# Where quarter B12 stands in the second pair of token tiles, and when the third sum of weights is formed

## What is computed

```python
def _L0_ffn_ref(x, W_base, b_base, W_gate, W_thr, b_thr, A_w, B_w):
    ...
    base = jnp.einsum('bsd,od->bso', x, W_base) + b_base
    xf = x.reshape(-1, D)
    gate = jax.nn.softmax(xf @ W_gate.T, axis=-1)
    thr = jax.nn.sigmoid(xf @ W_thr + b_thr[0]) * MAX_THRESHOLD
    adapted = gate - thr[:, None]
    selected = (adapted >= 0).astype(x.dtype)
    w = adapted * selected
    wsum = jnp.sum(w, axis=-1, keepdims=True)
    wsum = jnp.where(wsum == 0, jnp.ones_like(wsum), wsum)
    w = w / wsum
    h = jnp.einsum('nd,erd->ner', xf, A_w)
    moe = jnp.einsum('ner,ne,eor->no', h, w, B_w) * SCALING
    return base + moe.reshape(base.shape)
...
x = x + jnp.tanh(g_xattn[0]) * _L0_xattn_ref(_layernorm(x, axis=-1), ctx_4096, ...)
x = x + jnp.tanh(g_ffn[0]) * _L0_ffn_ref(_layernorm(x, axis=-1), ...)
```

## Time and profile before

| | us |
|---|---|
| median of three runs | 489.45 (488.79 to 489.53) |
| the profiled execution, its own time | 489.19 |
| its span, first to last instruction | 487.1 |
| PE busy in the span | 473.6 |
| DVE busy in the span | 345.9 |
| ACT busy, POOL busy | 164.6, 127.5 |

### The profile page before, as it was taken

The page is one execution under the profiler, slowest core; times in us unless marked ns, Lnnn a source line. Parts: engine busy times, 40 slices in busy tenths (PEclk is TensorE's granted clock), DMA queues, the critical chain, the costliest instruction groups (busy, mean ns, idle before and its releaser), DMA issues.

```text
span 487.1 us, 6840 instructions
## 1 busy us (share of the span) xinstructions
PE 473.6 (97%) x2460; PEld 402.2 (83%) x2460; DVE 345.9 (71%) x720; ACT 164.6 (34%) x338; POOL 127.5 (26%) x113
## 2 busy tenths in 40 slices
PE   4999999999999999999999999999999999999997
PEld 3888899998888888888888887877888888888885
DVE  1267758563787867769977996988767679777742
ACT  3765312310214204227326325244151422414300
POOL 1011011002353353336152515514040401305000
PEclk9999999999999999999999999999999999999999
DMA  8962262027843368557669035040503113050202
GB/s 291 412 247 87 88 250 96 1 87 253 266 137 123 150 215 283 199 200 249 208 257 399 4 131 215 27 146 2 172 3 129 45 60 113 1 173 1 86 0 87
DMA packets 20160, 71.80 MB, mean 147 GB/s; under 512 B 2464, under 2 KB 3488, under 8 KB 18848
## 3 DMA queue, kind: packets, MB, share of 16 engines
q1 hardware_dynamic: 19984, 71.35, 40.8%
q10 hardware_dynamic: 144, 0.02, 0.0%
HBM read 56.69 MB, written 14.68 MB: 147 GB/s over the span
## 4 chain that ended last, share of the span: by engine, by line
PE 79%; DVE 11%; issue 4%; DMA 3%; ACT 2%; POOL 0%; SPq 0%; DVEq 0%; ACTq 0%; POOLq 0%
PE bank L706 8%; PE bank L710 8%; PE bank L708 8%; PE bank L558 6%; PE bank L623 6%; PE bank L625 6%; PE bank L624 6%; PE bank L588 3%; PE bank L590 3%; PE bank L589 3%; PE bank L686 3%; PE bank L487 2%; DVE wl_T L1316 2%; DMA out_dram<-xs 2%; PE bank L609 2%
## 5 line engine op out<-in xcount | busy, mean ns | idle before, releaser
L1430 POOL TENSOR_TENSOR small<-small,tiny 128x1 f32<-128x1 f32 (+2 forms) x25 | 23.6, 945 | 150.3 <-DVE small L1079 124.1
L623 PE MATMUL bank<-xth,gram 128*128 128x512 f32 x144 | 57.4, 398 | 0.0
L625 PE MATMUL bank<-xtl,gram 128*128 128x512 f32 x144 | 56.3, 391 | 0.0
L624 PE MATMUL bank<-xth,gram 128*128 128x512 f32 x144 | 56.1, 390 | 0.0
L1404 DVE SCALAR_TENSOR_TENSOR xs<-bank,tiny,xs 128x512 f32<-128x512 f32 x56 | 40.2, 747 | 21.6 <-PE bank L710 15.7
L706 PE MATMUL bank<-wh_B,zh 128*128 128x512 f32 x136 | 55.2, 406 | 0.0
L710 PE MATMUL bank<-wh_B,zl 128*128 128x512 f32 x136 | 53.5, 393 | 0.0
L708 PE MATMUL bank<-wl_B,zh 128*128 128x512 f32 x136 | 53.3, 392 | 0.0
L1458 POOL TENSOR_TENSOR sq_sum<-sq_sum,sq 128x512 f32<-128x512 f32 x24 | 32.0, 1332 | 62.7 <-DVE sq L1252 62.7
L1494 POOL TENSOR_TENSOR xs<-xs,bb 128x1024 f32<-128x1024 f32 x16 | 39.5, 2468 | 10.3 <-ACT zn L946 7.7
L706 PE MATMUL bank<-wh_T,zh 128*128 128x512 f32 x96 | 39.3, 410 | 1.8 <-DVE wl_T L1316 1.6
(11 more groups left out here) (185 smaller groups left out, 1111.5 us busy)
## 6 DMA issues: line engine op xcount, KB each, us to landing
xst<-x_dram SPq DMA_DIRECT2D x16, 512.0 KB, 3.6
xz<-xt_dram SPq DMA_DIRECT2D x16, 512.0 KB, 6.8
out_dram<-xs SPq DMA_DIRECT2D x14, 512.0 KB, 3.0
xa<-x_dram SPq DMA_DIRECT2D x12, 512.0 KB, 3.3
x<-xa SPq DMA_DIRECT2D x12, 512.0 KB, 2.6
xs<-x SPq DMA_DIRECT2D x12, 512.0 KB, 4.0
wq_raw<-wq_dram SPq DMA_DIRECT2D x8, 512.0 KB, 14.9
wr_B<-wb_dram SPq DMA_DIRECT2D x4, 1024.0 KB, 8.5
```

Source lines behind the costliest of these rows:

```text
L623: pe.matmul(acc[:, :], gram[:, g, 0, :], xth[b % 2][:, r, :], start=r == ROWS[j][0], stop=False)
L624: pe.matmul(acc[:, :], gram[:, g, 1, :], xth[b % 2][:, r, :], start=False, stop=False)
L625: done = pe.matmul(acc[:, :], gram[:, g, 0, :], xtl[b % 2][:, r, :], start=False, stop=r == ROWS[j][-1])
```

## The change

Three things are edited, all of them in the list of stages or in the list of products.

- Pair 1 takes its eight products in the order 12a, 22a, 11a, 11b, 12b, 22b, 21a, 21b. Both products with B12 stand first, in places 0 and 1, where they stood in places 2 and 3.
- The load of T3 is a stage behind product 1 of pair 1 (it was behind product 3). The two sums of T3 on POOL are behind product 4 (they were behind product 7), and the first half's split behind product 6 of pair 1 (it was in pair 2, behind product 1). The second half's split is behind product 1 of pair 2 (it was behind product 2).
- In pairs 2 to 7 the choice of experts for the second tile is behind the first product and its partial sum (`part`), where it stood ahead of the products.

```diff
@@ -270,6 +270,7 @@
                           ("12a", "a11", "B12", "C", True), ("22a", "a21", "B12", "B", True),
                           ("12b", "a12", "B22", "C", False), ("22b", "a22", "B22", "B", False),
                           ("21a", "a21", "B11", "D", True), ("21b", "a22", "B21", "D", False)]
+        PLAIN_B12_FIRST = [PLAIN_PRODUCTS[n] for n in (2, 3, 0, 1, 4, 5, 6, 7)]
         PRODUCTS = [("P1", "a11", "B11", "A", True), ("P2", "a12", "B21", "B", True), ("P6", "s2", "T2", "A", False),
                     ("P5", "s1", "T1", "C", True), ("P7", "s3", "T3", "A", False), ("P3", "s4", "B22", "C", False),
                     ("P4", "a22", "T4", "D", True)]
@@ -283,7 +284,7 @@
             return p < PLAIN
 
         def products(p):
-            return PLAIN_PRODUCTS if plain(p) else PRODUCTS
+            return (PLAIN_PRODUCTS if p == 0 else PLAIN_B12_FIRST) if plain(p) else PRODUCTS
 
         def whole(p):
             return PLAIN_WHOLE if plain(p) else WHOLE
@@ -412,19 +413,21 @@
                          2: [("pt", 3), ("load_bt",), ("fn_split", 3)], 3: [], 4: [("sum", "T1", 0)],
                          5: [("mt", 1), ("fn_low", 3), ("sum", "T1", 1)], 6: [("bt",), ("sum", "T2", 0)], 7: [("sum", "T2", 1)]}
             else:
-                last += [("hd", p, 0), ("gates", t), ("hd", p, 1), ("gates", t + 1), ("chosen", t), ("chosen", t + 1)]
+                last += [("hd", p, 0), ("gates", t), ("hd", p, 1), ("gates", t + 1), ("chosen", t)] + [("chosen", t + 1)] * plain(p)
                 extra = {2: [("mt", t), ("mt", t + 1)]} if attends else {1: [("mt", t)], 2: [("mt", t + 1)]}
                 if plain(p):
                     extra = {0: [("split", "T1", 0), ("split", "T1", 1), ("sum", "T4", 0), ("sum", "T4", 1)],
-                             1: [("mt", t), ("mt", t + 1)], 2: [("split", "T2", 0)], 3: [("w_load", "T3")],
-                             4: [("split", "T2", 1)], 5: [("split", "T4", 0)], 6: [],
-                             7: [("sum", "T3", 0), ("sum", "T3", 1)]}
+                             1: [("mt", t), ("mt", t + 1), ("w_load", "T3")], 2: [("split", "T2", 0)], 3: [],
+                             4: [("split", "T2", 1), ("sum", "T3", 0), ("sum", "T3", 1)], 5: [("split", "T4", 0)], 6: [("split", "T3", 0)],
+                             7: []}
                 elif p == PLAIN:
-                    extra = {0: [("sum_low", p, "s4")], 1: [("mt", t), ("mt", t + 1), ("split", "T3", 0)], 2: [("split", "T3", 1)], 4: [("split", "T4", 1)]}
+                    extra = {0: [("sum_low", p, "s4")], 1: [("mt", t), ("mt", t + 1), ("split", "T3", 1)], 4: [("split", "T4", 1)]}
             for i, (name, *_) in enumerate(products(p)):
                 last.append(("prod", p, i))
                 if not plain(p) and name in PARTS:
                     last.append(("part", p, name))
+                    if i == 0:
+                        last.append(("chosen", t + 1))
                 last += extra.get(i, []) + ahead.get(i, [])
             for i in range(4):
                 last.append(("fin", p, i))
```

## The result

| | before | changed |
|---|---|---|
| median, us | 489.09 (488.74 to 490.19, 7 runs) | 491.31 (490.57 to 492.55, 7 runs) |
| ratio of the changed kernel to before | | 1.0043, 95% interval 1.0029 to 1.0057 |
| profiled execution, us | 489.19 | 490.57 |
| its span, us | 487.1 | 488.7 |
| mean granted clock of TensorE | 1.00 | 0.997 |

The change makes the kernel slower by 0.43%, about 2.1 us. The forecast was 490.7. The profiled execution of the changed kernel is the shortest of its seven; it is 1.4 us longer than that of before, and its span 1.6 us longer.

A forecast was written before the change was run, and what follows sets the result against it. PE was taken as the bound, busy 473.6 of 487.1 us. From 489.19, + 2.6 (head of pair 2) - 1.2 (P7) gave 490.6; with the median 0.26 higher, 490.7. Own range 490.1 to 491.3, whole range 488.1 to 491.4.

The forecast's parts named there:

- Part 1: Pair 1, B12 first: products cost nothing; T3's loads issue 3.1 us earlier, the second landing at 299 to 300.5.
- Rival A: T3 lands after 301.73, so its first POOL sum starts behind T2's split on DVE; 489.1 us, chance 0.12.
- Part 2: POOL's first T3 sum starts at 301.31 without waiting for the load, 0.94 us sooner and 0.42 ahead of T2's split.
- equal sharing: Alternative to whole turns: DVE and POOL at half rate while both busy, a12's low part 0.9 us later; 488.9 us.
- Part 3: T3's first split ahead of the tokens' low parts: a12's low part, and PE in pair 2's head, 2.6 us later.
- Rival B: DVE's queue is held no longer than before, third split free, only P7's gain left; 488.0 us, chance 0.18.
- Part 4: Choice of experts behind the part after P1: P6 waits for the second tile's expert weights instead; gain nothing.
- Part 5: P7's wait for T3's second split goes; the part after P6 then holds P7, so the gain is 1.24 us.
- rival C: PE's wait of some 3.1 us at 312.5 halves the clock for one product, adding 2.8 us; 493.4 us, chance 0.03.
- The list of waits: PE's waits behind the 7.1 us at the start: 1.6, 0.4 and 0.3 us, all in pair 2 and for DVE.

The follow-up runs named there:

- Run 3: Kernel before with only pair 1's products in the new order and T3's load behind the second of them; ratio 0.9998.
- run 1: Changed kernel with the split of T3's first half put back into pair 2, behind product 1; 488.18 us, ratio 0.9973.
- Run 5: Changed kernel with POOL's second sum of T3, and so the bias behind it, waiting for the low part of a12; 488.17 us, ratio 0.9975.
- run 2: Kernel before with only the second tile's choice of experts moved behind the part after P1 in pairs 2 to 7; ratio 0.9997.
- Run 6: Changed kernel with ten matmuls nobody reads put into PE's two waits in the head of pair 2; 490.68 us, ratio 1.0035.
- run 11: Kernel before with both POOL sums of T3 waiting for the low part of a12 and T3's second split right behind its first; 487.56 us, ratio 0.9951.
- run 7: Kernel of run 1 with both POOL sums of T3 waiting for the low part of a12; 487.15 us, ratio 0.9959.
- run 4: Changed kernel with the choice of experts put back ahead of the products; 491.66 us, ratio 1.0047.
- run 9: Kernel of run 7 with T3's sums waiting for s2's low part and the second tile's expert weights transposed behind product 2 of pair 2; 489.71 us.
- run 8: Changed kernel: T3's sums wait for s2's low part, both T3 splits in pair 2, second expert-weight transposes and second statistics later; 487.86 us.

## Why the prediction was right, and where it was not

The side and the mechanism came out as forecast. The median, 491.31, lies in the whole range (to 491.4) and 0.01 above the top of the forecast's own (491.3). By the steps:

- **Part 1**, the load: the second load was issued at 291.94 and took 7.5 us, so it landed at 299.4, in the 299 to 300.5 that was taken. Right. Rival A, which needed a later landing, did not occur. Run 3, the part alone, gives 0.9998.
- **Part 2**, POOL not held by the load any more, 0.42 us ahead of DVE: it came 0.47 us ahead (300.97 and 301.44). The turns were taken whole each time, in the three rows of 3.02, 3.42 and 3.40 us; equal sharing, which would have given 488.9, is not what they show. The Trainium skill (SBUF — State Buffer, "Who interferes with whom") says that such a pair blocks for the whole instruction. The three rows agree.
- **Part 3**, + 2.6 in the head: measured + 2.60, and run 1, which undoes this stage alone, takes back the head's wait and the loss with it. Run 5 shows that the turns are the reason, as the part says. Rival B, no longer hold than before, was the way things went only where POOL was made to wait.
- **Part 4**, nothing for the choice, with expert weights as the thing that P6 waits for: run 2 gives 0.9997 and exactly this wait (0.5 us). In the changed kernel itself P1 to P6 shrank by 0.50, since PE, slowed by its clock in the head, came later and met neither wait.
- **Part 5**, - 1.24 at P7, held by the part after P6: measured - 1.83. Run 1, where nothing delays the head, has - 1.19 and the named wait. Run 6 has the wait too, but it is not in the changed kernel, where PE came too late to meet it.
- **The clock**, costed at nothing, with 0.03 for rival C: this step failed. The half clock came, + 1.57 us on PE over the head rather than over a product. It was argued from the 1.6 and 7.1 us waits that show no lower clock, but the place in question has two waits with 1 us of small matmuls between them.
- **The list of waits** was read as if three stood behind the start. It has a fourth of such a size, the 0.5 us for `mtl` in pair 1, in the stretch whose products the change reorders. No term was given to it. It is gone in the changed kernel, but also in run 11, which has the old order, so that it is not shown to be the change's doing.

The misses of Parts 4 and 5 and that of the clock belong together. Run 6 is the forecast's own case, with the clock kept: against before, its P1 is + 2.64, its P6 + 2.85 and its P7 + 1.38 us, where the forecast had + 2.6, + 2.7 and + 1.4. The half clock adds 1.57 in front, and 0.50 + 0.59 of it come back in waits for DVE that PE no longer has. With - 0.30 at the start and + 0.06 at the end, these are the 1.6 us of the span. That the profiled execution, 490.57 us, falls on the 490.6 of the forecast's sum is therefore in part luck: of the 0.48 us that the half clock leaves, which the sum does not have, the - 0.30 of this execution hides a part, and its time grew by 1.4 us where its span grew by 1.6. The median came 0.6 us above the forecast.

The change moves the time as a sum of two parts of opposite sign, and only the runs part them: the second split's earlier place gives about 1.2 to 1.3 us (run 1, since runs 2 and 3 leave nothing for the other parts of it; it was not run alone), and the first split's place costs what lies between run 1's 0.9973 and 1.0043, 3.4 us. The forecast had 1.2 and 2.6 for them. The traces of run 1 and of the changed kernel, by the stretches of the table, give 2.95 us more to the head's first matmul with a12 (run 1 does not have the head's wait of 0.45 us that before has the earlier trace rows), 1.58 for the half clock, and 0.72 and 0.64 back at P6 and P7: 3.2 us together.

What stays open: the changed kernel's median lies 0.74 above its profiled execution. Six of its seven executions have the same mean clock of 0.997, so that the clock does not explain the spread among them, and nothing here does; the seventh has 0.992 and is the longest (492.55).

## What to carry to other kernels

When two engines take turns on a port, what an operation costs is read from its neighbour's queue: the same three splits took 5.3 or 9.7 us here. Work that is needed late (T3, first used 20 us later) is best kept from both queues until the operands that the bottleneck waits for next are made, and one wait on the lesser engine does it: 0.7% in the changed kernel (run 5), and 0.1% when it is added to run 1 (run 7), where the intervals overlap. A second loss on PE, such as its clock, is to be netted against the waits for others that it removes, and a stage that is moved later has to be followed through the banks it keeps.

## What the runs showed of the hardware that was not expected

The clock fell behind two waits of 0.97 and 1.82 us with 1 us of small matmuls between them (PE busy 1.31 of 4 us), and it stayed at half for 3.4 us in the changed kernel, with PE busy without a gap. In run 4 it fell already in the second wait and stayed at half for about 6.8 us, the last 5.8 of them with PE busy without a gap; there the head behind a12 took 5.39 us, where it takes 4.50 in the changed kernel and 2.93 before. A single wait of 1.6 us in the kernel before did not bring it down in its profiled execution, but the runs' clocks suggest that such waits can: the twelve executions of run 9, whose two longest waits in pair 2 are 1.6 us and less, fall into seven with a mean clock of 0.997 (489.58 to 491.11 us) and five with 0.999 or 1.000 (487.86 to 488.92), and three of the 23 executions of the kernel before in that session have 0.996 (491.01 to 491.86 us, median of all 490.01), though a fourth of these is as long (491.37) at 0.999. Run 9's program comes out some 1.8 us longer in the executions with the lower mean clock (medians of 489.88 and 488.11), and run 4's some 1.2 us longer in those with 0.992 or 0.993 (492.29 against 491.08). Only one execution of each kernel is profiled, so that the place of the drop in the others is inferred, and what decides whether it comes was not tried. In the changed kernel DVE's lateness hid a good part of what the half clock took.

POOL also holds an instruction of DVE that has one tensor and two values per partition as inputs. In run 8 the choice of experts for the first tile meets POOL's bias:

```profile
315.69 2.21 DVE L1380 TENSOR_SCALAR gsm<-gsm 128x8 f32<-128x8 f32 x1
```

```profile
315.48 2.40 POOL L1503 TENSOR_TENSOR xs<-xs,bb 128x1024 f32<-128x1024 f32 x1
```

The same instruction takes 0.29 us in the second tile (at 319.84), and here it ends 0.02 us behind POOL's. Run 9 shows the same (2.21 us, ending 0.03 us behind). The two-input splits and low parts of the prediction are therefore not the only work that waits for POOL.
